# Three latent attention loops: reciprocal ahead of the row maximum, output product ahead of the product over keys, scores in products of 256 columns

## The reference

```python
q_r = jnp.einsum('bshq,hqr->bhsr', q_big, W_qr)      # queries, through folded weights
k_r = jnp.einsum('bld,hdr->bhlr', kv_r, W_kr)
scores = jnp.einsum('bhsr,bhlr->bhsl', q_r, k_r)
attn = jax.nn.softmax(scores, axis=-1)
ctx_c = jnp.einsum('bhsl,bld->bhsd', attn, kv_r)     # product over keys
ctx_lat = jnp.einsum('bhsd,hkd->bhsk', ctx_c, w_kc_kv)
ctx = ctx_lat.transpose(0, 2, 1, 3).reshape(Bv, Sv, H * K)
return ctx @ Wo.T                                    # folded with the line before into one output product
```

## Time and profile before

| | |
|---|---|
| time, median of 3 runs | 2960.64 us (2959.87 to 2961.27) |
| the profiled execution | 2961.07 us, of which the span from first to last instruction is 2959.2 us |
| busy share of the span | PE 82%, DVE 59%, ACT 34%, POOL 26% |
| mean granted clock of TensorE | 0.869 |
| the three loops | 897 to 1140, 1999 to 2242 and 2517 to 2760 us of the span |

### The profile page before, as it was taken

How to read it: one execution, slowest core, us unless ns; L and a number is a source line. 1 busy time by engine, 2 the same in 40 slices (tenths; PEclk the granted TensorE clock), 3 DMA queues, 4 the chain that set the end, 5 groups by cost and what they waited for, 6 DMA issues and landing times. The chain is left out here.

```text
span 2959.2 us, 37118 instructions
## 1 busy us (share of the span) xinstructions
PE 2425.8 (82%) x14074; PEld 1610.9 (54%) x14074; DVE 1737.1 (59%) x3519; ACT 1008.2 (34%) x2293; POOL 769.9 (26%) x573
## 2 busy tenths in 40 slices
PE   7797343486999997977979797889998887999899
PEld 4555222123434555665858586755557765555555
DVE  5435678696435664278696969525665763565311
ACT  3032001362105552124545453415552131555210
POOL 1120001000007883300000000008881000888322
PEclk8788555697999998987888989789999969999999
DMA  1000000003000001041010101030001004000311
GB/s 35 19 21 22 0 0 14 0 0 107 1 0 1 1 1 58 1 147 27 30 29 30 29 30 29 2 100 1 1 1 43 21 1 100 1 1 1 118 36 39
DMA packets 98937, 81.29 MB, mean 27 GB/s; under 512 B 51504, under 2 KB 90272, under 8 KB 98185
## 3 DMA queue, kind: packets, MB, share of 16 engines
q1 hardware_dynamic: 97737, 77.47, 9.2%
q0 software_dynamic: 1024, 1.45, 0.2%
HBM read 73.56 MB, written 5.35 MB: 27 GB/s over the span
## 5 line engine op out<-in xcount | busy, mean ns | idle before, releaser
L2017 POOL TENSOR_SCALAR work<-work,small 128x512 f32<-128x512 f32 x384 | 594.3, 1566 | 706.6 <-DVE small L1952 705.3
L1995 ACT ACTIVATE work<-psum,small 128x512 f32<-128x512 f32 x384 | 260.6, 683 | 254.6 <-DVE small L1947 254.6
L1947 DVE TENSOR_REDUCE small<-psum 128x2 f32<-128x1024 f32 x192 | 234.7, 1224 | 176.0 <-PE psum L1897 176.0
L1907 PEld LDWEIGHTS psum<-consts,work 128*128 128x128 f32 x1536 | 165.4, 141 | 113.8 <-issue 102.1
L1897 PE MATMUL psum<-keysT,arena_a 64*128 64x512 f32 x768 | 219.2, 650 | 8.9 <-ACT work L1995 6.0
L1919 PE MATMUL psum<-work,keys 128*64 128x256 f32 x1536 | 187.0, 384 | 36.9 <-issue 34.3
L1907 PE MATMUL psum<-consts,work 128*128 128x128 f32 x1536 | 211.3, 281 | 3.5 <-DVE work L1958 2.6
L1919 PEld LDWEIGHTS psum<-work,keys 128*64 128x64 f32 x1536 | 120.0, 136 | 136.7 <-issue 110.8
L2849 PE MATMUL psum<-xnT,arena_a 128*128 128x256 f32 x512 | 138.2, 425 | 24.7 <-DVE arena_b L3269 23.8
L1958 DVE COPY work<-psum 128x512 f32<-128x512 f32 x192 | 130.9, 682 | 19.7 <-PE psum L1907 19.7
L2002 ACT ACTIVATE work<-psum 128x512 f32<-128x512 f32 x192 | 114.4, 596 | 71.8 <-PE psum L1907 71.8
(11 more groups left out here) (589 smaller groups left out, 4992.5 us busy)
## 6 DMA issues: line engine op xcount, KB each, us to landing
arena_b<-alpha_rows SPq DMA_DIRECT2D x16, 512.0 KB, 5.7
arena_a<-in_L_xattn_Wo SPq DMA_DIRECT2D x3, 2048.0 KB, 14.6
arena_a<-in_L_xattn_Wq SPq DMA_DIRECT2D x3, 2048.0 KB, 12.7
arena_a<-in_L_xattn_w_kc_q SPq DMA_DIRECT2D x3, 1536.0 KB, 12.2
arena_a<-in_L_attn_w_qkv SPq DMA_DIRECT2D x1, 4096.0 KB
arena_a<-in_L_xattn_W_qr SPq DMA_DIRECT2D x3, 768.0 KB
arena_b<-in_L_ffn_w_fc SPq DMA_DIRECT2D x1, 2048.0 KB
arena_b<-in_L_ffn_w_proj SPq DMA_DIRECT2D x1, 2048.0 KB
```

The lines of the kernel that those rows point to most:

```text
L1907: mm = nc.tensor.transpose(ps[:, 4 + j, c * P:(c + 1) * P], probs[u % NPB][:, j, c * P:(c + 1) * P], k.c["ident"])
L1947: nc.vector.tensor_reduce(top[:, 2 * u:2 * u + 2], ps[:, u % 2 * 2:u % 2 * 2 + 2, :], AX.X, ALU.max, negate=True).then_inc(*maxed.up())
L1995: nc.scalar.activation(probs[u % NPB][:, j, :], ps[:, u % 2 * 2 + j, :], ACT.Exp, bias=top[:, i:i + 1], accum_out=total[:, i:i + 1]).then_ ...
L2017: nc.gpsimd.tensor_scalar(probs[u % NPB][:, j, :], probs[u % NPB][:, j, :], total[:, i:i + 1], None, ALU.mult).then_inc(*scaled.up())
```

## The change

On TensorE, `scores` issues four products of 256 columns in place of two of 512: both heads for the first 256 keys, then both heads for the other 256. `output` of a couple moves from the end of an even iteration to the next odd one, behind that iteration's `scores` and ahead of the `over_keys` of the next couple. On VectorE, `invert(s-1)` stands ahead of `row_max(s)` in place of behind it, and `add` of a batch moves from the end of an even iteration to the end of the next odd one.

```diff
                 if u >= 2:
                     pe.wait_ge(*expd.at(2 * (u - 2) + 2))
-                for j in range(2):
-                    r = j * DC
-                    mm = nc.tensor.matmul(ps[:, u % 2 * 2 + j, :], qT[r:r + DC, p, t * P:(t + 1) * P],
-                                          k.keysT[r:r + DC, b * SK:(b + 1) * SK], start=True, stop=True)
+                for half in range(2):
+                    for j in range(2):
+                        r, at = j * DC, half * S
+                        mm = nc.tensor.matmul(ps[:, u % 2 * 2 + j, at:at + S], qT[r:r + DC, p, t * P:(t + 1) * P],
+                                              k.keysT[r:r + DC, b * SK + at:b * SK + at + S], start=True, stop=True)
                 mm.then_inc(*scored.up())
...
-            for s in range(U + LAG + 4):
+            for s in range(U + LAG + 6):
                 if s < U:
                     scores(s)
+                if s % 2 == 1 and 0 <= (s - LAG - 4) // 2 < U // 2:
+                    output((s - LAG - 4) // 2)
                 if s % 2 == 1 and 0 <= (s - LAG - 2) // 2 < U // 2:
                     over_keys((s - LAG - 2) // 2)
                 if 0 <= s - LAG < U:
                     turn(s - LAG)
-                if s % 2 == 0 and 0 <= (s - LAG - 3) // 2 < U // 2:
-                    output((s - LAG - 3) // 2)
...
             for s in range(U + LAG + 5):
+                if 0 <= s - 1 < U:
+                    invert(s - 1)
                 if s < U:
                     row_max(s)
-                if 0 <= s - 1 < U:
-                    invert(s - 1)
                 q = (s - LAG - 2) // 2
                 if s % 2 == 1 and 0 <= q < U // 2:
                     keep_sums(q)
                 if 0 <= s - LAG < U:
                     keep(s - LAG)
-                q = (s - LAG - 3) // 2
-                if s % 2 == 0 and 0 <= q < U // 2 and q % HP == HP - 1:
+                q = (s - LAG - 4) // 2
+                if s % 2 == 1 and 0 <= q < U // 2 and q % HP == HP - 1:
                     add(q // HP)
```

## The result

The changed kernel takes 2973.98 us (median of 5 runs, 2971.16 to 2979.08) against 2960.64 us (5 runs, 2958.35 to 2965.09): a ratio of 1.0048, with a 95% interval of 1.0035 to 1.0061. The medians are 13.3 us apart; the ratio is worked out from the single runs and not from the medians, and its interval is 10.4 to 18.1 us. Two executions of later experiments, of 5990.48 and 4800.66 us, fell far outside the rest and are left out of every comparison. The profiled execution took 2972.96 us with a span of 2971.1 us, 11.9 us more than the one of before.

The account below looks back on a forecast made before the run. The kernel was taken to be bound by a ring of releases across engines, 7.37 us a couple, not by TensorE's work. Opening +7.4 and `add` +5.9 gave +13.3 on 2961.07, 2974.4, less 0.43: 2974.0 us, range 2966 to 2986.

Parts of the forecast that it names:

- The ring: Even row maximum, exponentials, ScalarE's `keep`, `over_keys`, transposes and next scores release each other in turn: 7.37 us a couple.
- The rival that the earlier scaling matters: Transposes wait for GpSimd's scaling, so its earlier release could win 0.39 us a couple, 37 in all: 2937; chance 0.03.
- The opening, +7.4: Units 0 to 4: each row maximum now waits for the exponentials of the unit before; +7.4 us over three loops.
- The step of 2.81: Opening, one row maximum to the next: 1.26 to the exponentials, 1.48 to the reciprocal, 0.07 to what follows, in us.
- `add`, +5.9: VectorE at batch ends: `add` makes an even unit's row maximum 0.65 us late, nine times; +5.9 us.
- `output`, nothing: TensorE ahead of `over_keys`: one more change of weight shape, at most 0.12 us, fits in 0.39 of idle time; zero.
- one of the signs: In the changed profile, TensorE was to idle 0.3 to 0.4 us ahead of `over_keys`.
- The scores, nothing: Scores in products of 256 columns on TensorE: weight loads stay hidden; zero, between -10.4 and +20.9 us.
- loads that show: Rival: the extra weight loads of the split scores products are not hidden, +20.9 us, 2994.9; chance 0.08.
- shorter products: Rival: split scores products get shorter by at most 0.12 us each, -10.4 us, 2963.6; chance 0.07.
- The cold opening: Rival: more waits in the opening drop TensorE's clock for two units a loop, +5.5 us, 2979.5; chance 0.13.

Follow-up runs that it names:

- the reciprocal alone: Kernel before with only the reciprocal `invert(s-1)` put ahead of `row_max(s)` on VectorE; ratio 1.0035 (1.0022 to 1.0047).
- the scores alone: Kernel before with only the scores issued in four products of 256 columns; ratio 0.9999 (0.9990 to 1.0008).
- the products of 128 columns: Kernel before with the scores in eight products of 128 columns in place of two; ratio 1.0016 (1.0006 to 1.0025).
- output and add alone: Kernel before with only `output` moved ahead of `over_keys` and `add` to the end of the odd iteration; ratio 1.0037 (1.0023 to 1.0052).
- the kernel before with keep first: Kernel before with ScalarE's `keep` ahead of the exponentials in even iterations; two runs, 2928.93 us against 2964.54 and 2918.65 against 2960.13.

## Why the prediction was right

The forecast of 2974.0 met 2973.98; most of that closeness is luck: the five runs lie between 2971.16 and 2979.08, and the medians of the kernel before differed by up to 7 us between sessions. The steps have to be judged by the loops, where 13.3 was forecast and 12.4 measured.

*The ring.* Right, and shown from both sides: work put into it lengthens every couple by itself (8.28), and cutting it takes TensorE to its own pace (6.91). The rival that the earlier scaling matters fell with the reciprocal alone: couples of 7.37.

*The opening, +7.4.* Measured +7.36 in the changed kernel and +7.4 with the reciprocal alone. The step of 2.81 from three rows was exact to a hundredth, and that the new opening would be the same in all loops, while the old ones differed by 0.4, made the sum 2.62 + 2.55 + 2.24 and not three times the first.

*`add`, +5.9.* The mechanism was right and the size was off: 7.92 is 0.55 more than 7.37 where I had 0.65, so 4.9 in all. The step of the sum that was mis-sized is 1.39 + 0.07 - 0.81. I took the 0.81 of idle time as the room behind `keep`, which sets `add` at the recorded end of `keep`, and the next instruction on VectorE starts ahead of that end: `add` starts 0.61 after `keep` in the rows after, and `keep` is 0.69 long. The step from start to start would have given it.

*`output`, nothing.* Right in the changed kernel, since 0.39 of idle time covered it. Its price without that cover was too low: 0.20 a couple and not 0.12. It was 0.10 in two places, since the transposes, too, lost a neighbour with the same row groups. For the same reason one of the signs did not come: TensorE idles 0.19 ahead of `over_keys` and not 0.3 to 0.4.

*The scores, nothing.* Right: 1.13 or 1.14 a product, 0.004 us more a couple, 0.4 us in all. Both rivals, loads that show and shorter products, fell with the scores alone, and the products of 128 columns leave no room for the first.

*The cold opening.* A stretch at the lower clock did come, in all three loops: in the first, the granted clock of the changed kernel is 0.50, the 1.2 GHz level, from 901.9 to 905.9, and scores took 2.08 and transposes 1.97 there. It cost nothing in that kernel, where 5.5 us had been put on it, since unit 4 was reduced at 11.2 all the same; the new opening is set by VectorE and ScalarE and has room for slower scores. So the condition of this rival came true and its price was wrong. In the reciprocal alone it cost once, 0.25 us.

The single edits add up to 11.1 of the 12.4: 7.4, 3.7 and 0.0. Of the missing 1.3, 0.4 is in the openings. The old opening differs by some tenths from run to run, and in the profiles of the scores alone and of output and add alone it was 0.3 shorter in each, the three loops together, than in the kernel before; with the reciprocal alone the new one was 0.2 longer than in the changed kernel. The other 0.9 is in the couples behind the opening. A couple at a batch's end is 7.92 with all three edits and 7.86 without the reciprocal ahead of the row maximum, which makes 0.5 in nine; the last 0.4 are hundredths of a couple that stay open.

## What to carry to other kernels

Before an instruction is moved on an in-order engine, find the ring: follow one period of the loop through its releases until it comes back to the same instruction. Here work moved about outside the ring was free as long as what it added (0.20 us) fitted into the idle time there (0.39), and the same work inside the ring cost nearly its whole length in each period (0.91 of 0.96). Idle time on the busiest engine was here the sign of a ring through other engines. Then look at the two places that a steady period does not show, the opening, where an early wait turns a pipeline into a chain, and the iteration with something extra; and after moving two instructions of which one waits for the other, check that wait again: `output` and `add` each had room in their new places, but together they made a new wait of 0.59 us.

## What the runs showed of the hardware

The first loop of the changed kernel began at 896.38 us, and that of the reciprocal alone at 905.76, though the code ahead of it is the same in both. Within the loops the couples repeated to a hundredth of a microsecond, and the three loops of the two runs of the kernel before with keep first differ by 0.2 us together. Whole executions of the kernel before spread from 2952.74 to 2965.86 us in 15 runs on one chip. That this spread comes from other stages is likely, but none of those 15 was profiled; which stages, and why, was not looked into.

In these streams a new load of 128 weights into a row group whose products are running cost next to nothing: 12 more loads in a scores product made it 0.03 us longer, although the steps of 128 columns are only about 0.107 us and each has two loads.
